# Expert MLP pieces of half the size placed by VectorE's time; the last MLP's bias moved to GpSimd

## Chip, cores and metric

The kernel runs on one core of a Trainium2 chip. The metric is the device time of one execution in microseconds, start to end; lower is better. The engines are called as the profile calls them: PE is TensorE's matmul (PEld its weight loads), DVE is VectorE, ACT is ScalarE, POOL is GpSimd, SP is the engine that issues most transfers.

## The reference, cut to what matters

The program is a chain of blocks over 4096 rows of 256 numbers: a Mamba block, causal attention, a SwiGLU MLP, a routed mixture of 8 experts, banded attention and a last MLP with GELU, with layer norms between. Two blocks are touched by the change in earnest:

```
def balanced_assignment(scores):           # T = 4096 rows, E = 8 experts, C = 512 rows each
    taken = zeros(T, bool)
    for e in range(E):
        s = where(taken, -inf, scores[:, e])
        _, idx = top_k(s, C)               # expert e takes its best C rows of those left
        parts.append(idx); taken = taken.at[idx].set(True)
routed = feat[sort_by_expert].reshape(E, C, D)
h = gelu(layer_norm(routed) @ w1[e] + b1[e]) @ w2[e] + b2[e]      # 256 -> 1024 -> 256, per expert
out = (routed + h) put back in row order
...
h = gelu(x @ w1 + b1, approximate=False)   # the last MLP, 256 -> 1024 -> 256, all rows
x = layernorm(x + (h @ w2 + b2))
```

## The kernel before

Rows lie in 32 tiles of 128 (X), worked through in 8 chunks of 512 rows (NC = 8, TPC = 4 tiles each). Matmuls are in float32. The stages run one after the other with a barrier of all engines between them: Mamba, causal attention, SwiGLU MLP (stage_mlp, kind "swiglu"), routing with the experts (stage_route), banded attention, last MLP (stage_mlp, kind "gelu").

**Routing.** Expert e's 512 rows are found by a search on DVE, expert after expert, since each leaves out the rows taken before it. A search goes in 12 steps (ASKS); in each, DVE makes a small count per partition and *asks* PE to sum it over the partitions with a small matmul (tell, line 2417; ask, line 2257), then waits for the answer (the wait on told). The 12 are: four counting questions and a pick (take_above), again four and a pick, one for ties, one for ranks (rank_taken). Behind the rank DVE builds one-hot arrays (lines 2310 and 2316), POOL multiplies two of them (one_hots), PE turns them into the list of rows with 64 small matmuls ("ids", line 2448), DVE copies the list out (copy_ids), SP writes it to memory and reads it back as indices, POOL gathers the rows with four indirect transfers (gather), and PE may start the expert's MLP: 8 transposes ("turn"), 8 pieces "up" (each two matmuls of 512 columns, behind each a GELU on ACT), and for each of the four tiles of rows two pieces "down" (each four matmuls of 256 columns), whose sum DVE takes with the bias ("out", add_bias). SP loads an expert's weights when the MLP two experts before it is done, and only then passes to that expert's list.

So PE has two jobs at once: it answers the questions of one search and computes the MLPs of earlier experts. It takes its instructions strictly in the order of the program, and that order is made by hand in ExpertPlan (line 1963). Time there is counted in questions: expert e's MLP begins 7.5 questions into the search after its own and its 17 pieces are spread evenly over 12 questions. DVE runs the acts "copy" and "out" that the plan puts between two questions right behind asking and before it waits for the answer (meanwhile).

**The last MLP.** Per chunk, PE transposes (transpose, line 1905), does 8 "up" groups into two PSUM banks with a GELU on ACT behind each, transposes the next chunk, and does for each tile 8 matmuls of 256 columns and a ninth of one row, ones_row times b2, that adds the bias (line 1941). DVE copies the rows of X into hn ahead of each chunk (rows, line 1810), adds the MLP's result to X (line 1842) and does the layer norm's sums; ACT and DVE finish the norm one chunk later. Chunks are two written out, a loop over pairs (Fori), two written out (chunks, line 1653), in the SwiGLU MLP too. At the start PE waits for the biases, transposes them (line 1899), waits for both weights and only then transposes the first chunk.

Of the kernel before, what the change touches and what calls it, by code (L numbers as in the profile page):

```python
# [46 lines left out]
E = 8  # L47
# [1556 lines left out]
def stage_mlp(k, kind):  # L1604
# [11 lines left out]
    with ExitStack() as ctx:  # L1616
# [13 lines left out]
        if not swiglu:  # L1630
            nb = E if expert else 1
            b1r = sb(tag + "_b1r", [nb * NF, P], F32)
            b1 = sb(tag + "_b1", [P, nb * NF], F32)
            b2 = sb(tag + "_b2", [1, nb, D], F32)
            ones_row = sb(tag + "_ones", [1, P], F32)
        if not gelu:
            gb = sb(tag + "_gb", [P, 2, KD], F32)
        hn = sb(tag + "_hn", [P, 2, TPC, D], F32)
# [4 lines left out]
        (w_in, b_in, b_T, ones_set, hn_ready, hnT, hT_ready, up, silu, G_ready, down, x_sum, x_out,  # L1643
         var_ready, std_ready, renorm, freed, combined, stat) = k.sems(
            tag, "w_in b_in b_T ones hn_ready hnT hT_ready up silu G_ready down x_sum x_out "
# [19 lines left out]
        with nc.Block() as block:  # L1665
            @block.sync
            def _(sp):
# [26 lines left out]
                if gelu:  # L1694
                    sp.dma_start(b1r[:, :], a["L1_ffn_b1"].rearrange("(f p) -> f p", p=P))\  # L1695
                        .then_inc(b_in, 16)
                    sp.dma_start(b2[:, 0, :], a["L1_ffn_b2"].rearrange("(one d) -> one d", one=1))\
                        .then_inc(b_in, 16)
# [53 lines left out]
            def _(act):  # L1752
# [7 lines left out]
                if not swiglu:  # L1760
# [30 lines left out]
                transposed(0, 0)  # L1791
                chunks(act, body)
# [6 lines left out]
            def _(dve):  # L1799
# [10 lines left out]
                def rows(c, u):  # L1810

                    for j in range(TPC):
                        tile = TPC * c + j
                        if swiglu:
                            ins = normalised(dve, k, hn[:, u, j, :], tile)
                        else:
                            ins = dve.tensor_scalar(hn[:, u, j, :], X[:, tile, :], 1.0, None,  # L1817
                                                    ALU.mult)
                        ins.then_inc(hn_ready, 1)

                def body(c, it, u, first, last):
                    for f in range(NF):
# [4 lines left out]
                        if f == 3 and not last and not expert:  # L1827
# [3 lines left out]
                    for j in range(TPC):  # L1831
# [9 lines left out]
                        else:  # L1841
                            ins = dve.tensor_tensor(X[:, tile, :], src, X[:, tile, :], ALU.add)  # L1842
# [23 lines left out]
                if not expert:  # L1866
# [27 lines left out]
            def _(pe):  # L1894
                pe.sem_inc(down, 8)
                if not swiglu:
                    pe.wait_ge(b_in, 16 * (4 if expert else 2))
                    pe.wait_ge(ones_set, 1)
# [3 lines left out]
                if not expert:  # L1902
                    pe.wait_ge(w_in, 16 * (3 if swiglu else 2))

                def transpose(c, it, u):
                    if expert:
                        pe.wait_ge(rows_in[u], 16 * it + 16)
                    else:
                        pe.wait_ge(hn_ready, TPC * c + TPC)
                    for kd in range(KD):  # L1910
                        for j in range(TPC):
                            mm = pe.transpose(PS[:, 4 + kd, P * j:P * j + P],  # L1912
                                              hn[:, u, j, P * kd:P * kd + P], k.ident[:, :])
                        mm.then_inc(hnT, 1)

                def body(c, it, u, first, last):
# [17 lines left out]
                    for j in range(TPC):  # L1934
                        pe.wait_ge(x_out, TPC * c + j + 7)
                        dst = PS[:, 6 + j % 2, 0:D]
                        for f in range(NF):
                            mm = pe.matmul(dst, G[:, f, P * j:P * j + P], w2[u][:, f, :],  # L1938
                                           start=(f == 0), stop=(f == NF - 1 and swiglu))
                        if not swiglu:  # L1940
# [4 lines left out]
                transpose(0, 0, 0)  # L1945
                chunks(pe, body)
# [16 lines left out]
class ExpertPlan:  # L1963


    def __init__(self):
        acts = []
        for e in range(E):
            told = ASKS * (e + 1) if e < E - 1 else ASKS * (E - 1) + 1
            begin, unit = ASKS * (e + 1) + 7.5, ASKS / 17  # L1970
            acts += [(told + 2.5, "ids", e), (told + 2.6, "copy", e), (begin, "turn", e)]
            acts += [(begin + unit * (1 + f), "up", e, f) for f in range(NF)]
            for j in range(TPC):
# [574 lines left out]
```

## Time and profile before

| what | us |
|---|---|
| median of three executions (4169.05 to 4177.55) | 4175.17 |
| the profiled execution | 4178.09 |
| its span, first to last instruction | 4176.3 |
| of it the SwiGLU MLP, 2354 to 2717 | 363 |
| routing and experts, 2717 to 3169.6 | 452.6 |
| last MLP, 3896.9 to 4176.3 | 279.4 |

| busy in | PE | DVE | ACT | POOL | granted clock |
|---|---|---|---|---|---|
| whole span | 3479.3 (83%) | 2425.5 (58%) | 1680.8 (40%) | 1143.2 (27%) | 0.927 |
| SwiGLU MLP | 342.8 | 106.4 | 69.9 | 22.1 | 0.97 |
| routing and experts | 308.7 | 234.8 | 83.2 | 87.4 | 0.84 |
| last MLP | 259.8 | 50.9 | 71.6 | 0.2 | 0.96 |

The times are busy times of an engine within the stretch; a granted clock of 1.00 is 2.4 GHz at PE, 0.50 is 1.2 GHz. In the two MLP stages one engine, PE, is busy almost throughout. In the routing stage none is.

### The profile page before, as it was taken

The numbers are of one execution on the slowest core, as the hardware profiler recorded it, in microseconds if no ns is written. First come the engines' busy times: TensorE is split into PE (matmuls) and PEld (weight loads), VectorE is DVE, ScalarE is ACT, GpSimd is POOL, SyncE is SP. The second block draws the span as 40 slices with busy tenths as digits, with TensorE's granted clock in tenths as the row PEclk, the third lists the DMA queues.
The fourth block names the chain that finished last, engine by engine and source line by source line (L and its number), as shares of the span: only waits on it lengthen the run. The fifth ranks groups of instructions, "written<-read, shape, count | busy, mean of one in ns | idle before, by whom it ended". The sixth has DMA issues, their size and how long they took to land. (4 is left out here: it accounts for less than half of the span.)

```text
span 4176.3 us, 47591 instructions
## 1 busy us (share of the span) xinstructions
PE 3479.3 (83%) x17329; PEld 1741.4 (42%) x17329; DVE 2425.5 (58%) x4104; ACT 1680.8 (40%) x2670; POOL 1143.2 (27%) x975
## 2 busy tenths in 40 slices
PE   6889999986579989999899799938883778778799
PEld 2334433332233333333333265614551455456465
DVE  2999999999457767677677133265613233344212
ACT  4655555554214545555555412111122334334222
POOL 2667677667321001220000000001222223211000
PEclk9999999999879999999999899969996889889799
DMA  2222222222231111211120100021222854653100
GB/s 78 71 67 70 68 69 68 67 69 72 51 59 35 22 30 32 41 36 29 28 37 7 46 16 10 5 97 56 70 71 86 150 95 91 120 82 51 32 15 20
DMA packets 210060, 232.04 MB, mean 56 GB/s; under 512 B 58695, under 2 KB 160408, under 8 KB 208524
## 3 DMA queue, kind: packets, MB, share of 16 engines
q1 hardware_dynamic: 206764, 220.72, 23.0%
q0 software_dynamic: 3072, 8.39, 0.6%
q8 instruction: 134, 2.20, 0.2%
q14 instruction: 90, 0.74, 0.1%
HBM read 183.13 MB, written 45.89 MB: 55 GB/s over the span
## 5 line engine op out<-in xcount | busy, mean ns | idle before, releaser
L1365 DVE TENSOR_REDUCE g_mxp<-PS 128x1 f32<-128x512 f32 (+3 forms) x1280 | 722.6, 606 | 222.2 <-PE PS L1511 122.0
L1237 ACT ACTIVATE g_pT<-PS 128x1024 f32<-128x1024 f32 (+3 forms) x640 | 552.4, 894 | 474.6 <-PE PS L1526 279.1
L379 POOL TENSOR_TENSOR WB<-m_dtx,WB 128x1024 f32<-128x1024 f32 x256 | 601.0, 2351 | 294.3 <-DVE WB L523 260.1
L411 ACT ACTIVATE PS<-m_dt,m_A 128x512 f32<-128x512 f32 x512 | 353.1, 691 | 431.0 <-DVE WB L514 430.4
L1503 PE MATMUL PS<-g_KT,WB 96*128 96x512 bf16 (+3 forms) x1280 | 429.3, 363 | 105.9 <-DVE g_mxp L1365 92.9
L608 PE MATMUL PS<-WB,ident 128*128 128x512 f32 x1024 | 503.0, 615 | 0.0
L514 DVE TENSOR_TENSOR_SCAN WB<-PS,m_state,WB 128x512 f32<-128x512 f32 x384 | 469.9, 1263 | 14.9 <-ACT PS L411 14.8
L1526 PE MATMUL PS<-WB,g_KT 99*128 99x512 bf16 (+3 forms) x1280 | 358.1, 352 | 1.2 <-ACT g_pT L1237 0.6
L1503 PEld LDWEIGHTS PS<-g_KT,WB 96*128 96x128 bf16 x1280 | 116.9, 98 | 480.6 <-DVE g_mxp L1365 400.9
L523 DVE TENSOR_TENSOR WB<-WB,PS 128x1024 f32<-128x1024 f32 x256 | 306.2, 1196 | 7.2 <-DVE WB L514 2.6
L1545 PE MATMUL PS<-g_pT,WA 128*32 128x512 f32 (+3 forms) x2560 | 300.9, 542 | 0.6 <-ACT g_pT L1237 0.6
L1365 DVE TENSOR_REDUCE w_mxp<-PS 128x2 f32<-128x512 f32 (+1 forms) x256 | 170.8, 670 | 217.8 <-PE PS L1511 215.4
L1237 ACT ACTIVATE w_pT<-PS 128x512 f32<-128x512 f32 (+2 forms) x352 | 159.7, 470 | 307.9 <-PE PS L1532 307.4
L608 PEld LDWEIGHTS PS<-WB,ident 128*128 128x128 f32 x1024 | 201.2, 196 | 175.3 <-issue 164.3
L1927 PE MATMUL PS<-s_hT,WA 128*128 128x512 f32 x512 | 223.3, 597 | 1.0 <-ACT s_hT L1769 1.0
L594 PE MATMUL PS<-m_bc,m_sel 96*128 96x512 bf16 x256 | 100.3, 392 | 120.3 <-DVE WB L523 119.9
L1526 PE MATMUL PS<-WB,w_KT 99*128 99x256 bf16 (+2 forms) x704 | 143.4, 251 | 65.1 <-DMA WB<-w_dm 65.0
L1392 DVE TENSOR_TENSOR X<-X,PS 128x512 f32<-128x512 f32 x128 | 88.0, 687 | 173.7 <-PE PS L1565 173.6
L514 DVE TENSOR_TENSOR_SCAN WB<-PS,WB 128x512 f32<-128x512 f32 x128 | 149.0, 1204 | 23.5 <-POOL WB L379 16.8
L1526 PEld LDWEIGHTS PS<-WB,g_KT 99*128 99x128 bf16 x1280 | 119.0, 99 | 96.3 <-ACT g_pT L1237 26.1
L1207 POOL TENSOR_TENSOR g_On<-g_Ot,g_rden 128x512 f32<-128x512 f32 x32 | 40.6, 1269 | 409.8 <-DMA g_rden<-g_dn 409.8
L1503 PE MATMUL PS<-w_KT,WB 96*128 96x192 bf16 (+2 forms) x704 | 136.2, 257 | 19.2 <-DMA w_V<-w_dv 18.2
(309 smaller groups left out, 5360.2 us busy)
## 6 DMA issues: line engine op xcount, KB each, us to landing
WB<-b_rows SPq DMA_DIRECT2D x256, 256.0 KB, 3.2
WB<-in_L_ffn_w SPq DMA_DIRECT2D x18, 1024.0 KB, 7.6
WB<-g_dq SPq DMA_DIRECT2D x96, 128.0 KB, 3.9
WB<-w_dq SPq DMA_DIRECT2D x96, 128.0 KB, 7.7
w_KT<-w_dk SPq DMA_DIRECT2D x96, 128.0 KB, 8.4
g_rden<-g_dn SPq DMA_DIRECT2D x128, 64.0 KB, 2.0
w_dv<-WA SPq DMA_DIRECT2D x8, 1024.0 KB, 4.7
w_V<-w_dv SPq DMA_DIRECT2D x16, 512.0 KB, 12.1
```

The source lines that it names most:

```text
L379: pool.tensor_tensor(hh[:, g % RING, :, :], dtx[:, MB * h:MB * h + MB, :], Bs[:, g % BRING, :].unsqueeze(1) .broadcast_to([P, MB, CH]), AL ...
L411: act.activation(PS[:, 2 + b, :], dt[:, c % 2, m, :], ACT.Exp, scale=Aneg[:, n, m:m + 1]).then_inc(dA_ready, 1)
L514: dve.tensor_tensor_scan(hh[:, g % RING, b, :], PS[:, 2 + b, :], hh[:, g % RING, b, :], first, ALU.mult, ALU.add)\
L523: dve.tensor_tensor(hC[:, g % 2, :, :], hh[:, g % RING, :, :], PS[:, 4, :].unsqueeze(1).broadcast_to([P, MB, CH]), ALU.mult).then_inc(hc, 1)
L594: pe.matmul(PS[:, 4, :], sel[:, n, :], bc3[:, c % 2, :], start=True, stop=True)\
L608: mm = pe.matmul(PS[:, b, :], k.ident[:, :], hC[:, g % 2, b, :], start=False, stop=False, skip_group_check=True)
L1237: act.activation(pT[:, n % 2, 2 * pair:2 * pair + 2, 0:width], PS[:, 2 * pair:2 * pair + 2, at:at + width], ACT.Exp, scale=DH ** -0.5).the ...
L1365: dve.tensor_reduce(mxp[:, q % 6, i % QB, hh:hh + per, k0 // CH if causal else 0], PS[:, 4 + m % 2, :].rearrange("p (h n) -> p h n", h=per ...
L1503: mm = pe.matmul(bank[:, lo - k0:hi - k0], QT[0:KS, u % QRING, h, P * (i % QB):P * (i % QB) + P], KT[0:KS, region(s, lo // CH), kmap(h), l ...
L1526: mm = pe.matmul(bank[:, at:at + width], KT[:, region(s, j // QB), kmap(h), P * (j % QB):P * (j % QB) + P], QT[:, chunk(q) % QRING, h, at: ...
L1545: mm = pe.matmul(PS[32 * hh:32 * hh + 32, 6, at:at + width], V[:, region(s, j // QB), j % QB, kmap(4 * g + hh), :], pT[:, n % 2, hh, 0:wid ...
L1927: mm = pe.matmul(PS[:, bank, :], w[:, kd, P * f:P * f + P], hT[:, u, kd, :], start=(kd == 0), stop=(kd == KD - 1))
```

## The change

1. ExpertPlan counts in microseconds. The 12 questions of a search get distances of their own (2.6, 1.7, 2.9, ... 6.8; together 32.5); an MLP's pieces are spread over one such search by their length, starting 17.0 into the search after the expert's own; "ids" goes 8.2 behind the rank question. An "up" piece is one matmul of 512 columns (it was two), a "down" piece is two of 256 columns (it was four). The number of matmuls, questions and copies is the same.
2. In the last MLP the bias matmul and ones_row are gone. b2 is loaded broadcast to all partitions, and POOL adds it to X, tile by tile, once the chunk's transposes have read X; DVE's addition waits for that (x_sum).
3. In the last MLP PE transposes straight from X; DVE's copies into hn and the waits on them are gone.
4. In the last MLP and the SwiGLU MLP PE waits for the weights behind the first chunk's transposes instead of before them; in the last MLP the biases' transpose stands behind them too, and ACT waits for b1 only then.
5. In the same two stages the eight chunks are all written out, without a loop.

```
-            for u in range(2):
-                body(u, 0, u, u == 0, False)
-            with eng.Fori(1, NC // 2 - 1) as it:
-                for u in range(2):
-                    body(2 * it + u, it, u, False, False)
-            for u in range(2):
-                body(NC - 2 + u, NC // 2 - 1, u, False, u == 1)
+            for c in range(NC):
+                body(c, c // 2, c % 2, c == 0, c == NC - 1)
...
+                if gelu:
+                    pool.wait_ge(b2_in, 16)
+                    with pool.Fori(0, NC) as c:
+                        pool.wait_ge(hnT, KD * c + KD)
+                        for j in range(TPC):
+                            pool.tensor_tensor(X[:, TPC * c + j, :], X[:, TPC * c + j, :],
+                                               b2[:, 0, :], ALU.add).then_inc(x_sum, 1)
...
                         else:
+                            dve.wait_ge(x_sum, TPC * c + j + 1)
                             ins = dve.tensor_tensor(X[:, tile, :], src, X[:, tile, :], ALU.add)
...
-                        if not swiglu:
+                        if expert:
                             mm = pe.matmul(dst, ones_row[:, :], b2[:, c if expert else 0, :],
                                            start=False, stop=True)
...
                 transpose(0, 0, 0)
+                if gelu:
+                    small()
+                if not expert:
+                    pe.wait_ge(w_in, 16 * (3 if swiglu else 2))
                 chunks(pe, body)
...
+        step, pick = 2.6, 1.7
+        pace = [step] * (len(STEPS) - 1) + [pick, 2.9] + [step] * (len(STEPS) - 1) + \
+            [pick, 1.5, 2.3, 6.8]
+        slot = sum(pace)
+        begin = slot + 17.0
+        works = [("turn", 1.1)]
+        works += [("up", 0.86)] * (2 * NF)
+        works += [("down", 0.86)] * (4 * TPC)
+        whole = sum(w for _, w in works)
         for e in range(E):
...
+            told = slot * (e + 1) - pace[-1] if e < E - 1 else slot * (E - 1) + 1.0
+            acts += [(told + 8.2, "ids", e), (told + 8.3, "copy", e)]
+            p, count = begin + slot * e, {}
+            for what, w in works:
...
+                p += w * slot / whole
...
-                        e, f = x
-                        if f == 0:
+                        e, f, kd = x
+                        if f == 0 and kd == 0:
...
-                        for f in range(NF // 2 * h, NF // 2 * h + NF // 2):
+                        for f in range(NF // 4 * h, NF // 4 * h + NF // 4):
                             mm = pe.matmul(PS[:, 6 + j % 2, 0:D], G[:, f, P * j:P * j + P],
```

## Rows read from the trace of the kernel before

**Rows 1.** windows of the searches and two after (us, busy by engine, PEclk, DMA)
```profile
core 0: us, PE busy (x) PEld busy (x) DVE busy (x) ACT busy (x) POOL busy (x), PEclk, DMA share, GB/s
2767.87:2797.43 29.56, 3.21 (x15) 2.07 (x15) 23.03 (x77) 0.00 (x0) 1.15 (x1) 0.50 0.00 0
2797.43:2834.96 37.53, 19.59 (x111) 10.26 (x111) 24.44 (x78) 6.27 (x8) 7.15 (x7) 0.61 0.05 15
2834.96:2875.11 40.15, 33.28 (x184) 20.98 (x183) 25.60 (x81) 6.94 (x10) 6.88 (x7) 1.00 0.21 66
2875.11:2917.80 42.69, 36.16 (x184) 22.16 (x183) 25.60 (x81) 6.94 (x10) 10.80 (x11) 0.92 0.22 74
2917.80:2959.10 41.30, 34.78 (x184) 21.52 (x183) 25.59 (x81) 6.94 (x10) 11.26 (x11) 0.96 0.24 77
...
3000.50:3041.80 41.30, 34.75 (x184) 21.61 (x183) 25.61 (x82) 6.94 (x10) 10.79 (x11) 0.96 0.23 77
3041.80:3068.57 26.77, 23.54 (x203) 17.64 (x203) 6.71 (x17) 2.06 (x3) 11.96 (x12) 0.94 0.11 31
```
**Rows 2.** timeline of PE behind the last question (start us, length us, ..., [idle])
```profile
3068.57 1.04 PE L2378 MATMUL PS<-ident,r_hn 128*128 128x128 f32 x8
3070.71 14.00 PE L2465 MATMUL PS<-r_hT,WB 128*128 128x512 f32 x32 [1.10 <-ACT r_hT L2173]
3085.49 14.08 PE L2476 MATMUL PS<-WB,WA 128*128 128x256 f32 x64 [0.78 <-ACT WA L2178]
3099.41 1.04 PE L2378 MATMUL PS<-ident,r_hn 128*128 128x128 f32 x8
```
**Rows 3.** timeline of PE between questions of one search, not consecutive
```profile
2838.06 0.18 PE L2433 MATMUL PS<-r_count,r_onesb 128*128 128x15 bf16 x1 [2.96 <-DVE r_count L2275]
...
2843.19 2.00 PE L2476 MATMUL PS<-WB,WA 128*128 128x256 f32 x8 [0.78 <-ACT WA L2178]
...
2845.12 0.19 PE L2448 MATMUL PS<-r_hot_col,r_hot_own 128*17 128x32 bf16 x1
...
2846.82 1.99 PE L2476 MATMUL PS<-WB,WA 128*128 128x256 f32 x8
```
**Rows 4.** timeline of DVE: questions of the first search and the same ones
```profile
2769.95 0.23 DVE L2276 TENSOR_SCALAR r_hit<-PS,r_one 128x15 f32<-128x15 f32 x1 [0.29 <-PE PS L2433]
...
2772.31 0.23 DVE L2276 TENSOR_SCALAR r_hit<-PS,r_one 128x15 f32<-128x15 f32 x1 [0.29 <-PE PS L2433]
...
2835.96 1.35 DVE L2269 SCALAR_TENSOR_TENSOR r_reach<-r_key,r_one,r_grid 128x480 bf16<-128x480 f32 x1
...
2838.95 0.72 DVE L2269 SCALAR_TENSOR_TENSOR r_reach<-r_key,r_one,r_grid 128x480 bf16<-128x480 f32 x1
...
2845.24 0.23 DVE L2276 TENSOR_SCALAR r_hit<-PS,r_one 128x15 f32<-128x15 f32 x1 [2.53 <-PE PS L2433]
```
**Rows 5.** timeline of SP and PE: an expert's list and its first use
```profile
2807.67 0.25 SPq L2091 DMA_DIRECT2D r_listed<-r_ids  x1
...
2817.76 1.97 PE L2378 MATMUL PS<-ident,r_hn 128*128 128x128 f32 x8 [0.88 <-DMA r_hn<-sorted,r_idx]
```
**Rows 6.** timeline of PE in the final MLP, end of the first chunk
```profile
3935.51 3.72 PE L1938 MATMUL PS<-WB,f_G 128*128 128x256 f32 x16
3939.79 3.72 PE L1938 MATMUL PS<-WB,f_G 128*128 128x256 f32 x16
3944.06 14.00 PE L1927 MATMUL PS<-f_hT,WB 128*128 128x512 f32 x32
```
**Rows 7.** timeline at the start of the final MLP
```profile
3896.88 0.91 SPq L187 DMA_DIRECT2D WB<-in_L_ffn_w  x2
...
3905.12 0.27 PE L1899 MATMUL PS<-ident,f_b1r 8*128 8x8 f32 x1 [21.42 <-DMA f_b<-in_L_ffn_b]
...
3909.17 17.02 PE L1927 MATMUL PS<-f_hT,WB 128*128 128x512 f32 x32 [0.69 <-ACT f_hT L1767]
```
**Rows 8.** line 1726 of the SwiGLU MLP (min/median/max ns)
```profile
L1726 POOL TENSOR_TENSOR s_io<-s_io,X x32: 722/725/730, 2367.1 to 2635.3; 128x256 f32<-128x256 f32 x32
```

More of the change, by code:

```diff
@@ L1759, in _ @@
                     act.wait_ge(b_in, 16 * (4 if expert else 2))
-                if not swiglu:
+                if expert:
                     act.wait_ge(b_T, 2)
@@ L1826, in body @@
                                               ALU.mult).then_inc(G_ready, 1)
-                        if f == 3 and not last and not expert:
+                        if f == 3 and not last and swiglu:
                             rows(c + 1, 1 - u)
@@ L1864, in renormalise @@
                         dve.wait_ge(renorm, TPC * c + TPC)
-                if not expert:
+                if swiglu:
                     rows(0, 0)
@@ L1895, in _, with small @@
                 pe.sem_inc(down, 8)
-                if not swiglu:
-                    pe.wait_ge(b_in, 16 * (4 if expert else 2))
-                    pe.wait_ge(ones_set, 1)
+                def small():
+                    pe.wait_ge(b_in, 16 * (4 if expert else 1))
+                    if expert:
+                        pe.wait_ge(ones_set, 1)
                     pe.transpose(PS[:, 7, 0:nb * NF], b1r[:, :], k.ident[0:nb * NF, 0:nb * NF])\
@@ L1901, in _ @@
                     pe.wait_ge(b_T, 2)
-                if not expert:
-                    pe.wait_ge(w_in, 16 * (3 if swiglu else 2))
+                if expert:
+                    small()
                 def transpose(c, it, u):
@@ L1938, in body @@
                             mm = pe.matmul(dst, G[:, f, P * j:P * j + P], w2[u][:, f, :],
-                                           start=(f == 0), stop=(f == NF - 1 and swiglu))
-                        if not swiglu:
+                                           start=(f == 0), stop=(f == NF - 1 and not expert))
+                        if expert:
                             mm = pe.matmul(dst, ones_row[:, :], b2[:, c if expert else 0, :],
@@ L1966, in __init__ @@
     def __init__(self):
-        acts = []
-        for e in range(E):
[L1969 to L1973, printed above, removed]
-                acts += [(begin + unit * (9 + 2 * j + h), "down", e, j, h) for h in range(2)]
-                acts.append((begin + unit * (10 + 2 * j) + 0.05, "out", e, j))
-        acts += [(g, "ask", g) for g in range(ASKS * (E - 1) + 1)]
+        step, pick = 2.6, 1.7
+        pace = [step] * (len(STEPS) - 1) + [pick, 2.9] + [step] * (len(STEPS) - 1) + \
+            [pick, 1.5, 2.3, 6.8]
+        assert len(pace) == ASKS
+        slot = sum(pace)
+        acts, at = [], 0.0
+        for g in range(ASKS * (E - 1) + 1):
+            acts.append((at, "ask", g))
+            at += pace[g % ASKS]
+        begin = slot + 17.0
[3 more added lines that the diff above has]
+        whole = sum(w for _, w in works)
+        for e in range(E):
+            told = slot * (e + 1) - pace[-1] if e < E - 1 else slot * (E - 1) + 1.0
+            acts += [(told + 8.2, "ids", e), (told + 8.3, "copy", e)]
+            p, count = begin + slot * e, {}
+            for what, w in works:
+                i = count[what] = count.get(what, -1) + 1
+                if what == "turn":
+                    acts.append((p, "turn", e))
+                elif what == "up":
+                    acts.append((p, "up", e, i // 2, i % 2))
+                else:
+                    acts.append((p, "down", e, i // 4, i % 4))
+                    if i % 4 == 3:
+                        acts.append((p + 1.0, "out", e, i // 4))
+                p += w * slot / whole
         self.order = [a[1:] for a in sorted(acts, key=lambda a: a[0])]
```

45 lines of the change are left out of this document (23 added, 22 removed).

## The prediction

> **What bounds the kernel now.** I read three views in this order: busy time and granted clock by stretch, to see which engine is full in which stage; the timelines of PE and DVE within one search, to see who waits for whom; and the last MLP's timeline. The profiled execution took 4178.09 us (span 4176.3), 2.9 above the median of 4175.17; the sum below is made against the former and then moved to the latter.
>
> In the last MLP PE is the bound: its matmuls follow each other without a gap [rows 6], so every matmul taken away there shortens the end by its own length. In the routing stage nobody is full. The first search, with no MLP beside it, takes 29.56 us; the one with the first MLP's beginning 37.53; then they take 40.15, 42.69 and three times 41.3 to 41.4 (the first and the last stand there), with DVE busy only 25.6 and PE 33 to 36 of it [rows 1]. The reader is to see the pattern in the rows: undisturbed, a question is answered 0.29 after DVE asked and the questions are 2.36 apart; with an MLP beside it DVE stands 2.53 for the same answer [rows 4], since PE works off "down", "ids" and the rest in program order first [rows 3]. A little before, PE stood 2.96 waiting for a question [rows 3]. Each waits for the other in turn. Behind the last question an MLP takes PE 30.84 us [rows 2], so neither engine needs 41.
>
> **The plan, part by part.** *Prices.* An "up" group of two matmuls is 14.00/8 = 1.75 us, and the piece of one half of it; I take 0.86. The 32 "down" matmuls of an MLP take 13.92, a quarter-tile piece 0.87; a turn is 1.04, behind it PE waits 1.10 for ACT, and 0.78 before the first "down" for the last GELU [rows 2] (counted from the matmul's issue 1.3 and 1.0). "ids" is 1.70 (from 2845.12 to 2846.82) [rows 3]. The work is unchanged; halving the pieces adds no instruction, and the semaphore counts stay.
>
> *Walk of a steady search.* I sorted the new plan's times and set PE's pieces in each gap beside what DVE needs in it. DVE's gaps, from question to question, are those of the first search's twelve, all within the 29.56 of its row: 2.36 between counting questions, 1.5 to a pick, 2.8 behind it, 1.2 to the ties, 2.6 to the ranks, about 7 to the next search. The new pieces: in the 7 us gap seven "up" (6.0, fits). Between the first and the second question one "up", the 1.0 for the GELU, a "down", "ids" and a "down": 0.86 + 1.0 + 0.87 + 1.70 + 0.87 = 5.3 against 2.36, an excess of 2.9. Then two "down" (none); three against 2.36 (0.3); two against 1.5 (0.3); three against 2.8 (none); two (0.1); two and the turn, 2.8 against 2.36 (0.4); two "up" behind the turn's wait of 1.3, 3.0 against 1.5 less what PE was early (0.7); two against 1.2 (0.3, and 0.7 for the ties' answer, which also waits); two against 2.6 (0.1). These are 5.1 to 5.8, I take 5.1 beyond the free answers, as the early question carries over. To this comes what POOL costs DVE: beside POOL's one-hot work the first step of a search takes 1.35 where the same step later takes 0.72 [rows 4], and the one before it is stretched alike: 1.25. So the new search is 29.56 + 1.25 + 5.1 = 35.9. DVE's four additions and the copy lie behind asking, under the answer, as now.
>
> The same walk with the old plan gives excesses of 9.0 and 39.8, where the one search at full clock took 40.15 [rows 1]; I add the missing 0.4 and get 36.3. Bounds: nothing below 29.56 + 1.25 = 30.8, which would need every question free; above, the 40.15 of today, if the waits only change places.
>
> *Clock.* Of the searches only the one of 40.15 had a granted clock of 1.00; in the others it was 0.92 to 0.96 [rows 1], which is PE at 1.2 GHz for a part, and each is 1.1 to 2.5 longer. The idle of 2.96 before the first question [rows 3] comes with it, though it stood ahead of the search at 1.00 too. In the new order PE has no gap over about 1.3 in a search, so I take these losses as gone. TensorE: Matmul & The Clock Gate (the Trainium skill), section "HAM oscillation", says that a matmul engine left waiting between bursts falls back to half rate and pays the rise anew each time. By that rule the loss goes with the gaps, as in the sum; if instead it stayed as in these rows, the five searches would be some 7 longer.
>
> *Sum of the routing stage.* Five searches: 40.15 + 42.69 + 41.30 + 41.40 + 41.30 = 206.8 against 5 x 36.3 = 181.5: -25.3. The one before them carries the first MLP's beginning with a clock of 0.61 [rows 1]; it keeps that and gains what the walk gives, -3. Behind the last search, the time to the next turn was 26.77, with PE at 0.94 [rows 1]; now it is the last "up" pieces and question (3.4), 0.86 + 1.0, sixteen "down" (13.9) and two "ids" (3.4): 22.6, -4. Two whole MLPs of 30.84 follow unchanged, and the stage's end. Together -32.5.
>
> *What must come in time.* From SP's write of a list to the gathered rows at PE it takes 2817.76 - 2807.67 = 10.1 us [rows 5]. In the new plan the copy is about 14 before the turn; 4 are left. For the seventh expert I get 2.7. SP passes to a list behind the load of weights issued some 16 earlier, POOL's scatters are two experts old: both hidden. If a list were later, PE would stand at the turn with the questions behind it, 1 us for 1 us.
>
> **The last MLP.** Four matmul groups of a chunk start 4.28 apart with the bias (3935.51 to 3939.79) [rows 6]; without one, 13.92/4 = 3.48 [rows 2]. So 0.80 x 32 tiles = -25.6. What is late next: nothing, as the groups' sums have two banks and DVE takes one in less than half a us; the GELUs run as now. POOL's four additions a chunk, at 0.725 each [rows 8], start when the chunk is transposed and are done in 2.9, where the first "down" sum comes 3.5 behind its own "down" start and a whole "up" phase of 14 [rows 6] lies between for all but the wait's first chunk; there b2 lands with the biases around 3905 and the sum is due some 17 later. DVE is busy 51 of 279 in this stage, so what POOL's port use costs it is covered.
>
> *Starts.* PE begins now at 3905.12 when the biases are in, and the "up" matmuls at 3909.17 [rows 7]. With copies, transposes and ACT ahead of the loads, 3905.7 is possible: -3.5. But the rise to full clock, which cost the first chunk 17.02 - 14.00 = 3.0 [rows 6, 7], may then start as late as the matmuls: between 0 and -3.5 is kept, more by +1.5; I take -2.3. The SwiGLU MLP's first transposes (2 us at that clock) likewise move ahead of its weights, though ACT still waits for the norm's columns behind them: 0 to -3, taken -1. Loops written out save under 0.1 a chunk: -0.6. The removed DVE copies were hidden by PE: 0.
>
> **Sum.** -32.5 - 25.6 - 2.3 - 1 - 0.6 = -62. On the profiled execution 4178.1 - 62 = 4116; on the median, 4175.2 - 62 = 4113.
>
> **Rivals.** (a) *The searches run at DVE's pace.* If the excess at "ids" is smaller than walked, a search comes to 32.5, near the sum of the plan's own distances: 5 x 3.8 more, 4094. For it: PE's need per search is 28.9 + 1.7 and the answers, about 32.5. Against it: "ids" and the GELU's wait fall into one short gap. (b) *The waits change places.* Pieces twice as fine still stand ahead of questions; if the clock still falls and each search stays at 39 to 40, the routing stage gives about 10 and the whole 4136. For it: PE is needed nearly 90% of the new search, so any lateness stays. (c) *Slower: the list comes late.* If a list needed more than the 14 us that the plan leaves, PE stands at each of seven turns. The price is its lateness times seven; it decides from 62/7 = 9 us beyond the margin, a list of 23 us where the row shows 10.1. At 12 us beyond, 4175 + 22 = 4197. (d) *The change doesn't do what it says in the last MLP*: the sum on DVE waits for POOL each time, as POOL waits for the transposes of the same chunk. Only if POOL took over 14 a chunk; rows say 2.9. It would give 4139.
>
> **How the numbers follow.** My forecast (4100 to 4127) 0.66; (a) 0.10; (b) 0.18; (c) 0.03; (d) 0.03. The likeliest is 4113. The range takes in (a) and (b) with the bounds of the starts and the clock: 4092 to 4138. A measurement of this kernel tells about 0.2% (8 us) from no change; faster by more holds in all but (c) and a bad (b): 0.95, within 0.02, slower 0.03.
>
> **What the changed profile would show.** Searches of about 36 with a granted clock of 1.00 and PE busy near 90%; DVE's longest wait, about 3, at the second question; no wait of PE for gathered rows except at the first MLP. In the last MLP, no row of line 1941, chunks of 28.7 instead of 31.9, and DVE waiting for PE, not POOL, at its sums. The prediction is wrong if PE stands at turns, if the clock in the searches stays at 0.96, or if a chunk of the last MLP is over 29.

## The result, and the profile after

The changed kernel takes 4116.92 us (median of four executions, 4114.76 to 4124.66); the kernel before took 4176.36 beside it on the same chip (4169.05 to 4188.65). The ratio is 0.9859, with a 95% interval of 0.9838 to 0.9879. The profiled execution took 4114.76, its span is 4112.9 and its mean granted clock 0.931 (0.927 before). Forecast were 4113.

Where the time went is best read by stage. Each stage is measured from its own first transfer issue to that of the next, in the profiled executions (so the routing stage before is 2722.39 to 3169.66, less than the rounder stretch of the section on the time before):

| stage | before | after | change | the prediction's step |
|---|---|---|---|---|
| all up to the SwiGLU MLP's first load | 2353.9 | 2353.1 | -0.8 | none |
| SwiGLU MLP | 368.5 | 368.2 | -0.3 | -1 |
| routing and experts | 447.3 | 422.5 | -24.8 | -32.5 |
| banded attention (not touched) | 727.2 | 720.1 | -7.1 | none |
| last MLP | 279.4 | 249.1 | -30.3 | -28.5 |

First the windows over the seven searches, as in [rows 1]; the last two rows are the stretch from the last search to the next turn, and one whole MLP.

```profile
core 0: us, PE busy (x) PEld busy (x) DVE busy (x) ACT busy (x) POOL busy (x), PEclk, DMA share, GB/s
2765.60:2795.15 29.55, 3.22 (x15) 2.06 (x15) 23.02 (x77) 0.00 (x0) 1.18 (x1) 0.50 0.00 0
2795.15:2828.82 33.67, 18.97 (x112) 10.04 (x113) 24.45 (x78) 6.28 (x8) 7.08 (x7) 0.64 0.06 16
2828.82:2865.12 36.30, 33.24 (x185) 20.88 (x184) 25.77 (x82) 6.95 (x10) 7.00 (x7) 1.00 0.23 73
2865.12:2902.78 37.66, 33.42 (x185) 20.91 (x184) 25.75 (x82) 6.95 (x10) 10.84 (x11) 1.00 0.25 84
2902.78:2940.27 37.49, 33.42 (x185) 20.90 (x184) 25.83 (x82) 6.94 (x10) 10.91 (x11) 1.00 0.25 85
...
2977.78:3015.21 37.43, 33.37 (x184) 20.86 (x183) 25.83 (x81) 6.95 (x10) 10.85 (x11) 1.00 0.25 85
3015.21:3042.66 27.45, 23.78 (x204) 18.02 (x203) 6.76 (x17) 2.06 (x3) 12.75 (x12) 0.94 0.13 40
3042.66:3073.49 30.83, 28.95 (x106) 19.01 (x104) 1.70 (x4) 6.95 (x10) 10.70 (x11) 1.00 0.34 116
```

The searches that took 40.15 to 42.7 now take 36.3 and four times about 37.5, PE is busy 33.2 to 33.4 of them and its clock is 1.00 in each. The first of the five is the 36.3 of the prediction; the other four are 1.2 longer, and the stretch behind the last search is not shorter than before (27.45 for 26.77). Both are followed up below.

Next VectorE's timeline at the second question of that first search (start us, us, engine line op, tiles; in brackets the idle time ahead and what ended it), the place where the walk put its largest excess:

```profile
2832.11 0.23 DVE L2304 TENSOR_SCALAR r_hit<-PS,r_one 128x15 f32<-128x15 f32 x1 [0.28 <-PE PS L2461]
...
2833.54 0.66 DVE L2303 TENSOR_REDUCE r_count<-r_reach 128x15 bf16<-128x480 bf16 x1
2836.67 0.18 DVE L2266 CAST r_ids<-PS 17x32 uint32<-17x32 f32 x1 [2.48 <-PE PS L2476]
2837.74 0.23 DVE L2304 TENSOR_SCALAR r_hit<-PS,r_one 128x15 f32<-128x15 f32 x1 [0.89 <-PE PS L2461]
...
2840.09 0.23 DVE L2304 TENSOR_SCALAR r_hit<-PS,r_one 128x15 f32<-128x15 f32 x1 [0.28 <-PE PS L2461]
```

The question is asked at 2834.20 and answered at 2837.74: 3.5 us, against 0.28 for the first and the third question. DVE's copy of the ids between them shows the reason: PE was at "down", "ids" (L2476) and "down" first.

The last MLP, its start (PE's timeline) and its sums (groups of DVE and POOL):

```profile
3872.12 0.27 PE L1902 MATMUL PS<-ident,f_b1r 8*128 8x8 f32 x1 [6.16 <-DMA f_b1r<-in_L_ffn_b]
3872.66 16.48 PE L1932 MATMUL PS<-f_hT,WB 128*128 128x512 f32 x32 [0.26 <-DVE f_b L1814]
```

```profile
L1844 DVE TENSOR_TENSOR X<-PS,X 128x256 f32<-128x256 f32 x32 | 13.5, 422 | 92.4 <-PE PS L1943 92.4
L1720 POOL TENSOR_TENSOR X<-X,f_b 128x256 f32 x32 | 22.2, 732 | 196.7 <-PE PS L1917 169.7 <-DMA f_b<-in_L_ffn_b 27.1
```

The first "up" starts 8.8 us behind the stage's first load where it started 12.3 behind it [rows 7]; DVE's sums wait for PE alone. From the second on, the chunks start 28.6 apart where they were 31.9 apart.

### The profile page after: what moved, and what is told of

The parts are those of the page before. It is cut to its first block and busy times, and to the rows that moved or that the text cites. A ratio compares the mean times of both kernels' runs of the same rounds, so it can differ in the third digit from the quotient of the medians.

```text
span 4112.9 us, 47062 instructions
## 1 busy us (share of the span) xinstructions
PE 3444.2 (84%) x17265; PEld 1730.6 (42%) x17265; DVE 2419.5 (59%) x4072; ACT 1681.5 (41%) x2670; POOL 1166.4 (28%) x1006
## 5 line engine op out<-in xcount | busy, mean ns | idle before, releaser
L1932 PEld LDWEIGHTS PS<-s_hT,WA 128*128 128x128 f32 x512 | 98.3, 192 | 129.1 <-issue 128.8
```

What stands on the lines that cost most here:

```text
L1932: mm = pe.matmul(PS[:, bank, :], w[:, kd, P * f:P * f + P], hT[:, u, kd, :], start=(kd == 0), stop=(kd == KD - 1))
```

## The experiments

All edits are to the changed kernel unless said otherwise. "Routing stage" is from its first load to that of the banded attention, in the run's profile; the median of all the run's executions stands beside it, with that of the kernel before in the same comparison.

**1. One part at a time.** The plan with the MLP stages as before:

> The routing stage as in the changed kernel, all MLP stages as before. Theory (the two parts add up, and the plan is worth what the traces of the stage show): the stage takes 422 to 424 us where the kernel before had 447.3, searches of 37.5 at a granted clock of 1.00, the last MLP stays at 279 and the time is 4176.4 - 25 = 4151. The banded attention behind it, which the change doesn't touch, was 727.2 in the kernel before and 720.1 in the changed one. If those 7.1 belong to the plan (the stage finds PE in another state), they come here too and the time is 4144. If they are chance from one execution to the next, they can be here or not in the profile, and the time stays near 4151. Rival (the parts help each other through the clock or the loads): the gain is under 20.

Measured: 4144.31 (before 4177.66; ratio 0.9912, 0.9891 to 0.9933), routing stage 422.4, last MLP 279.2. The MLP stages with the plan as before:

> The MLP stages as in the changed kernel, the plan of the experts as before. Theory: the last MLP takes 249 instead of 279.4, the SwiGLU stage 368.2, searches stay at 40 to 43 with a clock of 0.92 to 0.96; the time is 4176.4 - 30.3 - 1 = 4145. If the 7.1 of the banded attention belong to the MLP stages, 4138. Rival: part of the 30.3 came from what PE had done before, then under 25 here, 4151 or more.

Measured: 4139.38 (ratio 0.9904, 0.9881 to 0.9927), routing stage 451.5, last MLP 249.1, SwiGLU stage 368.3.

By the stages the parts add up: 24.9 and 30.3, and the changed kernel has 24.8 and 30.3. By the medians they are 33.4 and 38.3, together 71.7 where the changed kernel gains 59.4; each of the three has an interval of 8 to 10 us to either side, so the medians neither confirm nor refute the sum. The routing stage of the old plan, the same instructions, took 447.3 in one execution and 451.5 in this one, so this stage is not known better than to some 4 us either. The banded attention, the same instructions in all of them, took 727.2, 720.1, 715.6 and 718.1 in these four profiled executions, and 716.9 to 730.2 in the ten below, with no order by kernel. So its -7.1 is nobody's gain, and from here on the stages decide and the medians only back them.

**2. The time axis or the half size?** Two kernels with the MLP stages as before; each has one part of the new plan. The first keeps the time axis and puts both halves of a piece at one place:

```diff
-        works += [("up", 0.86)] * (2 * NF)
-        works += [("down", 0.86)] * (4 * TPC)
+        works += [("up", 1.72)] * NF
+        works += [("down", 1.72)] * (2 * TPC)
...
-                    acts.append((p, "up", e, i // 2, i % 2))
+                    acts += [(p, "up", e, i, kd) for kd in range(2)]
...
-                    acts.append((p, "down", e, i // 4, i % 4))
-                    if i % 4 == 3:
-                        acts.append((p + 1.0, "out", e, i // 4))
+                    acts += [(p, "down", e, i // 2, 2 * (i % 2) + h) for h in range(2)]
+                    if i % 2:
+                        acts.append((p + 1.86, "out", e, i // 2))
```

> The plan's time axis with pieces of the old size (two matmuls of an up, four of a down at one place); MLP stages as before. Theory A (the axis does it): what stands ahead of a question is settled by the sum of the work in a gap; a walk of PE and DVE with the prediction's prices gives 36.0 per search where the half pieces give 35.9, so searches of 37.5 and the same time as with half pieces, within 3 us. Theory B (the size does it): a whole piece stands 0.86 us longer ahead of a question, at about half of the twelve questions of a search: 4 to 5 us a search more, 41 to 42, no gain over the kernel before and 20 to 25 slower than the half pieces.

The second lays half pieces evenly over the questions' numbers, as the old plan did with whole ones; "ids", turn and questions stand as in the old plan:

```diff
+            begin, unit = ASKS * (e + 1) + 7.5, ASKS / 17
+            for f in range(NF):
+                acts += [(begin + unit * (1 + f + kd / 2), "up", e, f, kd) for kd in range(2)]
+            for j in range(TPC):
+                acts += [(begin + unit * (9 + 2 * j + h / 2), "down", e, j, h) for h in range(4)]
+                acts.append((begin + unit * (10.5 + 2 * j) + 0.05, "out", e, j))
...
```

> Half pieces laid out evenly by the number of the question, as before, not by time; MLP stages as before. Theory A (the axis does it): about as many pieces stand in the gap of 1.5 us as in that of 7, the walk gives 39.1 per search plus 0.4, so 39.5 at full clock and up to 41.5 where the clock falls in the long gap; the time is 4168 to 4176. Theory B (the size does it): searches of 37.5 and the time of the half pieces on the time axis, about 4151.

Measured: whole pieces on the time axis 4149.1 (ratio 0.9925, 0.9898 to 0.9951) with a routing stage of 420.3; half pieces on the question axis 4176.14 (ratio 0.9999, 0.9983 to 1.0015) with one of 451.8. One steady search of each, in windows with the columns above:

```profile
2909.62:2946.04 36.42, 33.02 (x184) 21.04 (x183) 25.61 (x81) 6.95 (x10) 11.73 (x11) 1.00 0.27 87
```

```profile
2958.60:3000.00 41.40, 34.90 (x183) 21.61 (x183) 25.78 (x84) 6.97 (x10) 11.61 (x11) 0.96 0.23 77
```

The axis (with the ids' place on it) is the whole gain of the plan; halving the pieces alone gives nothing. Whole pieces on the time axis took 420.3 for 422.4, but no answer was late in their profile (experiment 5), and late answers cost the halves 4.8: without late answers a search with half pieces takes 36.3, one with whole pieces 36.4. The change's title names the half size first; the prediction gave it no price of its own, and the walk had not needed it. What counts is how much work stands in a gap beside the gap's length. The clock goes with it: in the second kernel, with more idle time of PE, it is 0.96 as in [rows 1].

**3. The bias back on TensorE**, with the rest of the last MLP as changed:

```diff
-                        if expert:
+                        if not swiglu:
                             mm = pe.matmul(dst, ones_row[:, :], b2[:, c if expert else 0, :],
                                            start=False, stop=True)
...
```

POOL's additions and DVE's wait for them are out, and ones_row is back.

> The changed kernel with the last MLP's bias added by TensorE's matmul again, in everything else as changed (order of the last MLP's start, transposes read from X, loops written out). Theory: each of the 32 tiles costs 0.80 us of TensorE again, chunks of 31.8 instead of 28.6, the last MLP takes 249.1 + 25.6 = 274.7, and of the difference to the kernel before (279.4) the rest of 4 to 5 is the start and the loops; the time is about 4117 + 25.6 = 4142. Rival (the bias matmul was cheaper than the 0.80 read off the starts, and the start and the loops gave more): under 20 more than the changed kernel, below 4137.

Measured: 4145.01 (before 4180.26; ratio 0.9910, 0.9896 to 0.9923), last MLP 275.1. PE's timeline in it:

```profile
3900.18 3.72 PE L1938 MATMUL PS<-WB,f_G 128*128 128x256 f32 x16
3903.83 0.69 PE L1941 MATMUL PS<-f_b,f_ones 1*128 1x256 f32 x2
3904.45 3.72 PE L1938 MATMUL PS<-WB,f_G 128*128 128x256 f32 x16
```

So the bias is 275.1 - 249.1 = 26.0 (0.81 a tile), and the start with the loops 279.2 - 275.1 = 4.1.

**4. The lists' margin.** The turns 8 us of the plan's time earlier (`begin = slot + 9.0` for 17.0):

> The changed kernel with each MLP's turn laid 8 us (of the plan's time) earlier against the searches: begin = slot + 9 for slot + 17. The prediction's margin for the list was 4 us. Theory (the list's way of about 10 us is the limit, and the questions stand in the queue behind TensorE's wait): TensorE waits 3.7 us for the gathered rows at each turn, the walk gives 39.1 instead of 35.9 per search, the routing stage 18 longer; with 1.2 a search of late answers gone or not, 4130 to 4140. Rival (the wait is covered by the slack of the answers): searches of 37.5 stay and the time within 4 us of 4117. If the list takes longer than 10.1, more by its lateness times seven.

Measured: 4166.27 (ratio 0.9962, 0.9945 to 0.9979), routing stage 472.0, 49.5 longer, searches of 45.7 to 47.2. One search in windows, and PE's timeline in it:

```profile
2922.04:2968.60 46.56, 37.15 (x185) 22.82 (x184) 25.95 (x82) 7.07 (x10) 11.19 (x10) 0.85 0.21 69
```

```profile
2936.21 1.11 PE L2504 MATMUL PS<-WB,WA 128*128 128x256 f32 x4
2944.64 1.97 PE L2406 MATMUL PS<-ident,r_hn 128*128 128x128 f32 x8 [7.32 <-DMA r_hn<-sorted,r_idx]
2946.40 0.23 PE L2453 MATMUL PS<-r_pick,r_onesb 128*128 128x32 bf16 x1
```

PE stands 7.3 at the turn, not 3.7, with the question of L2453 behind it. SP's queue tells why:

```profile
2930.48 0.25 SPq L2119 DMA_DIRECT2D r_listed<-r_ids  x1
2931.74 0.35 SPq L2122 DMA_DIRECT2D r_idx<-r_listed  x1
2937.35 0.38 SPq L2106 DMA_DIRECT2D WB<-in_L_ffn_w  x1
2937.77 0.47 SPq L2107 DMA_DIRECT2D WB<-in_L_ffn_w  x1
```

From the list's write to the rows at PE it is 2944.64 - 2930.48 = 14.2, not the 10.1 of [rows 5]: the load of 2 MB of weights, which now goes out before the gathered rows are in, runs beside the gathers. The same run tells it apart from the scatters: its first list, with no load beside it, took 9.9 (2796.91 to 2806.82), its second, with a load but before the first scatter, 13.8. And behind the idle time the clock is 0.85, so the pieces in front of the next questions take longer. Both costs were missing in the theory; the direction and the mechanism (the questions behind the waiting turn) were right. The cliff that the prediction's rival (c) spoke of is real, and 8 us of the plan's time away it costs 49.5, not 18. Rival (c)'s price, the lateness once for each of seven turns, fits: PE's seven waits there are 5.0 to 9.3 long and add up to 51.7.

**5. The late answers.** In each of the four searches of 37.5 two answers come late, the sixth and the seventh. DVE's timeline at the sixth question of one of them, then POOL's and PE's:

```profile
2957.94 0.66 DVE L2303 TENSOR_REDUCE r_count<-r_reach 128x15 bf16<-128x480 bf16 x1
2960.03 0.23 DVE L2304 TENSOR_SCALAR r_hit<-PS,r_one 128x15 f32<-128x15 f32 x1 [1.43 <-PE PS L2461]
```

```profile
2956.59 1.01 POOL L2158 DMA_INDIRECT hidden<-r_io,r_idx  x1 [0.30 <-issue]
2957.90 0.99 POOL L2158 DMA_INDIRECT hidden<-r_io,r_idx  x1 [0.30 <-issue]
2959.19 0.97 POOL L2158 DMA_INDIRECT hidden<-r_io,r_idx  x1 [0.30 <-issue]
```

```profile
2958.66 0.18 PE L2461 MATMUL PS<-r_count,r_onesb 128*128 128x15 bf16 x1
2958.69 1.97 PE L2504 MATMUL PS<-WB,WA 128*128 128x256 f32 x8
```

PE's matmul for that question starts at 2958.66, 0.06 behind the question's end, and takes 0.18; the answer is used 1.37 after its start where 0.22 is usual. PE was not late, and it went straight on with the next "down"; the signal was late. The trace's semaphore record says so itself: the update that DVE waits for is stamped 2960.00, and that of the "down" matmul ahead of the question, which started at 2958.37, came with it (2959.97). It happens while POOL issues an expert's scatters, the indirect transfers that put its results back, which exist from the fourth search on. The scatters moved behind the one-hot work:

```diff
-                    if e >= 3:
-                        scatter(e - 3)
                     if e < E - 1:
                         one_hots(e)
+                    if e >= 2:
+                        scatter(e - 2)
...
```

> The changed kernel, with GpSimd's four scatter transfers of an expert issued behind the one-hot work of the search before, about 10 us before they stand now, and so no longer straight behind the four gathers. In the changed kernel, from the fourth search on, TensorE's answer reaches VectorE 1.4 to 1.6 us after its matmul's start where it takes 0.22 elsewhere, while those scatters are issued; that is 1.2 us a search, and the last list's matmuls are slowed in the same way. Theory A (the row of eight indirect transfers on GpSimd delays TensorE's semaphore updates): the late answers are gone, searches of 36.3, the stage behind the last search 5 us shorter, in all 8 to 10 us less in the routing stage, 412 to 414 instead of 422.5. Theory B (each scatter delays what is signalled just then, wherever it stands): the late answer moves to another question, searches of 37.5 stay. Theory C (it has nothing to do with GpSimd): questions 6 and 7 stay late as they are.

Measured: 4116.49 (ratio 0.9841, 0.9826 to 0.9856), routing stage 419.1, the four searches 36.6 to 36.7 with no late answer. The second question waits 0.4 longer, since the ids beside a scatter take 2.1 for 1.76. So moving them took the lateness away, as theory A said, in this one profile. The stretch behind the last search is as long as it was, against theory A, so that of its 8 to 10 us 3.4 came.

There the last ids are slow. PE's groups between 3029.6 and 3034.1 of the changed kernel:

```profile
L2476 PE MATMUL PS<-r_hot_col,r_hot_own 128*17 128x32 bf16 x32 | 2.2, 176 | 0.9 <-issue 0.9
L2476 PE MATMUL PS<-r_hot_col,r_hot_tile 128*17 128x32 bf16 x32 | 2.1, 176 | 1.2 <-issue 1.2
```

They were laid later:

```diff
-            acts += [(told + 8.2, "ids", e), (told + 8.3, "copy", e)]
+            late = 0.0 if e < E - 1 else 12.0
+            acts += [(told + late + 8.2, "ids", e), (told + late + 8.3, "copy", e)]
```

> The changed kernel with only the last expert's ids (64 short matmuls) and their copy laid 12 us later, behind the turn of the seventh expert. In the changed kernel they took 4.37 us where the other seven took 1.76, with four indirect transfers issued by GpSimd in the same time; in other runs 2.1 with one beside them and 5.5 with five. That is what kept the stretch from the last search to the next turn at 27.45 where the prediction had 22.6. Theory A (GpSimd's indirect transfers slow TensorE's short instructions): the ids take 1.76 again, and the stretch loses their 1.7 (moved) and the stalls: 3015 to 3042.7 becomes 23 to 24; the routing stage is 2.5 to 3.5 shorter, since the ids' own 1.8 come back behind the turn. Theory B (two blocks of ids stand too near each other for the supply of instructions): here they are 18 us apart, the same result, but with the first downs of that stretch slow as well. Theory C (the place in the stage, whatever stands there): still 4 us or more. The whole time changes by less than its runs differ, so the trace decides.

Measured: 4106.6 (before 4172.99; ratio 0.9833, 0.9811 to 0.9855), routing stage 412.5, 10.0 less. The same group, and a window from the last search on, which runs 3.4 past the next turn:

```profile
L2477 PE MATMUL PS<-r_hot_col,r_hot_own 128*17 128x32 bf16 x32 | 1.7, 176 | 0.0
```

```profile
3010.23:3034.00 23.77, 21.89 (x150) 16.81 (x149) 7.06 (x17) 3.51 (x5) 12.74 (x12) 1.00 0.20 52
```

The ids take 1.76 again and the next turn (3030.65) comes 20.4 behind the last search for 27.45; 1.76 of the 7 come back behind it. That was more than expected, since the clock there is 1.00 for 0.94, too. Theory B of this run, two blocks of ids too near each other, is ruled out by the kernel before: its last two blocks start 5.9 apart (8.8 in the changed kernel) and took 1.76 and 1.75. Unexpected: all four searches took 36.35 with no late answer, with the scatters in their old place. Whether the ids' place did it was asked by a second execution of that routing stage, with the MLP stages as before:

> The run with the last ids laid 12 us later had searches of 36.35 without one late answer, although the scatters stand where they stood in the changed kernel (37.5). This is the same routing stage once more, with the MLP stages as before, so a second execution of the same stage. Theory A (the place of the last ids decides, by what lies in TensorE's and GpSimd's programs): 36.35 again in every search, a routing stage of 412 to 413. Theory B (the late answers come and go with the execution, as they were 0.7 to 1.6 in three executions of the changed plan): at least one search of 36.8 to 37.5, the stage 413 to 417. In both the last ids take 1.76, for no transfer of GpSimd stands beside them; the time 4176 - 35 = 4141 to 4137 by the medians.

Measured: 4146.73 (before 4177.12; ratio 0.9932, 0.9906 to 0.9957), routing stage 417.8, the four searches 37.49 to 37.65, and the last ids 1.76. Its median gives nothing away, as the runs spread by 21 us. So theory A is out: the same routing stage, instruction for instruction, had no late answer in one profile and late answers in all four searches in the other. Whether they come and go with the execution, as theory B has it, or with what else the program holds, is not shown, for each kernel was profiled once. The last ids, in their new place, took 1.76 in both.

**6. The walk as a planner.** Other distances in the time axis, found by trying many axes in the prediction's walk:

```diff
-        pace = [step] * (len(STEPS) - 1) + [pick, 2.9] + [step] * (len(STEPS) - 1) + \
-            [pick, 1.5, 2.3, 6.8]
+        pace = [1.6, 2.75, 2.75, 1.35, 3.45, 2.7, 1.5, 2.4, 1.55, 1.8, 2.5, 7.0]
-        begin = slot + 17.0
+        begin = slot + 15.9
-            acts += [(told + 8.2, "ids", e), (told + 8.3, "copy", e)]
+            acts += [(told + 7.5, "ids", e), (told + 7.60, "copy", e)]
```

> The changed kernel with other numbers in its time axis only: the distances between the questions of a search are 1.6, 2.75, 2.75, 1.35, 3.45, 2.7, 1.5, 2.4, 1.55, 1.8, 2.5, 7.0, the ids come 7.5 behind the last question instead of 8.2, and the turn 15.9 into the slot. They were found by running the prediction's walk of TensorE and VectorE over many such axes and keeping the one that ends first. Theory (the walk is right, the excess of 3.3 us at the second question is only the placing of ids): searches of 33.1 + 0.4, with no answer over 1.1 us late, the routing stage 15 us shorter, 4100 to 4103. Rival A (late answers of 1.2 us a search stay and grow with the stage's density): 4105 to 4108. Rival B (the walk fitted the shown order only, and what it can't see takes the place of the removed waits): searches stay at 36 to 37.5, 4112 or more.

Measured: 4099.87 (before 4180.26; ratio 0.9806, 0.9792 to 0.9819), routing stage 410.0, the first steady search 33.58, the four others 34.6 to 34.75 with the late answer. The median is next to the theory's 4100, but the stage is 12.5 shorter where the theory had 15: the walk's search came true (33.5 forecast), and so did the late answers of rival A. Then all three edits, and all but the moved scatters:

> The changed kernel with three edits together: the tuned distances of the run before, the scatters moved off the gathers, and the last ids late. Theory (they add up): searches of 33.5 with no late answer, where the tuned distances alone had 34.6; four searches by 1.1, and 3 behind the last one: the routing stage 402 to 403 where the tuned distances alone had 410.0, and 7 less in time, 4093. Rival (the scatters, now beside the ids of each expert, cost there what they cost at the answers: in the run with the scatters moved each block of ids took 2.1 for 1.76 and the second question waited 0.4 longer): searches of 33.9 to 34.2, the stage 405 to 407, 4096.

> The tuned distances with the last ids late, but the scatters where the changed kernel has them: the version with all three edits (routing stage 397.2, searches of 33.58) less the moved scatters. If the scatters' place is what makes TensorE's answers late, searches of 34.6 come back in at least some of the four from the third on and the stage takes 399 to 402. If it was the last ids, or nothing is left of the lateness in this order, 33.6 throughout and 397 to 398. The time is within 4 us of the version with all three, 4087.

Measured: all three 4086.93 (before 4172.99; ratio 0.9804, 0.9790 to 0.9817), routing stage 397.2, 5 to 6 less than expected, since the stretch from the last search to the next turn fell by 8.5 (27.8 to 19.3), of which 3 were counted on. The rival did not come: with scatters beside them the ids took 1.76 here, not 2.1. Without the moved scatters 4098.01 (before 4177.12; ratio 0.9810, 0.9782 to 0.9837), routing stage 405.1, longer than the 399 to 402 expected; its four searches are 34.7 to 34.9. A steady search of the version with all three:

```profile
2925.08:2958.65 33.57, 32.52 (x184) 21.31 (x183) 25.69 (x82) 6.94 (x11) 11.12 (x10) 1.00 0.29 95
```

PE is busy 32.5 of 33.6; this order is at PE's pace. It is the fastest of all, 86 us below the kernel before and 23 to 30 below the changed one (23 by the two ratios, 30 by the medians; the routing stage is 25.3 shorter).

## Why the prediction was right, point by point

The time was right (4113 for 4116.92, 3.9 off; 62 less forecast, 59.4 less measured), and so was the mechanism in both parts. A part of the closeness is luck. In the profiled executions the stages that the change touches gave 55.4 of the 62, as two terms of the routing stage were wrong, and 7.9 that no step had came from stages that the change doesn't touch (7.1 of it the banded attention), so that the whole came to 63.3. None of the prediction's signs of being wrong showed: no turn waited, the clock in the searches was 1.00, a chunk of the last MLP took 28.6.

- **What bounds each stage**: right. By the stages the two parts are independent (experiment 1).
- **The steady search, 36.3**: right for the order as walked. 36.30 where no scatter runs, 36.35 in an execution without late answers, 3.3 of excess at the second question (3.54 less the free 0.28) where 2.9 was walked, and PE busy 33.2 of 36.3, the "near 90%". The same walk, with its 0.4 added, forecast other orders: 36.4 (36.4 to 36.5 measured; the expectation on record said 37.5, as it took the late answers in) and 33.5 (33.58) at full clock. Where the clock fell it was short: 39.5 (41.3 to 43.8) with half pieces on the question axis, and 39.5 (45.7 to 47.2) with the turns earlier, where the list's way was too short in it as well. The four searches with scatters beside them were 1.2 longer, because their answers' signals came late. That term was missing: 4.8 in sum.
- **Clock, losses taken as gone**: right, 1.00 in all five. In experiments 2 and 4, where PE was left waiting, it was 0.96 and 0.85. That a matmul engine left waiting between bursts goes back to half rate is what TensorE: Matmul & The Clock Gate (the Trainium skill), section "HAM oscillation", states, and the traces agree in both directions.
- **The search before them, -3**: 37.53 to 33.67, -3.9.
- **Behind the last search, 26.77 to 22.6**: wrong, 27.45. The step priced the second ids at 1.7, from a row without POOL's transfers beside it. They took 4.4, and the clock fell to 1.2 GHz for a while behind their stalls (at 3034.6), which makes the stretch's mean 0.94. With them out of the way the same pieces took 20.4 (22.6 less the ids' 1.7 is 20.9). These 4.9 and the 4.8 above are more than the 7.7 that the stage's sum was too large; the search before the five and the stage's ends gave the difference back.
- **The list's margin of 4**: held in the changed order, where PE never waits for gathered rows. But 10.1 was read from a list with no load of weights beside it; where the two meet it is 13 to 15 (experiment 4). The chance of 0.03 for rival (c) rested on a number that the change itself could have moved.
- **The bias, -25.6**: -26.0. Rival (d), DVE waiting for POOL, is ruled out by the row of L1844: all its 92.4 of waiting is for PE.
- **The last MLP's start, -2.3, and the loops, -0.6**: together -4.1 for -2.9. The first "up" comes 3.5 earlier against the stage's first load, as held possible, and the first chunk's 16.48 is no longer than the 17.02 of [rows 7]: the clock's rise was not paid a second time, so all of the 3.5 was kept.
- **SwiGLU, -1**: -0.3 in this pair of profiles, which one pair can't tell: the stage took 366.7 to 369.1 in the fourteen, 368.0 on average in the nine with this change and 368.8 in the five without. The transposes go first, but ACT's wait for the norm's columns sets the start, as the prediction named for the lower end.
- **Rival (a), DVE's pace**, did not come: the best order run here took 33.6 with PE busy 32.5 of it, so the rival's 32.5 would leave PE no wait at all. **Rival (b)** did not come as told, for the clock held and no search took 39. But lateness did take back 9.7 of the 32.5 that the prediction expected from the stage, by signals and stalls and not by pieces ahead of questions.

## What to carry to other kernels

Where two engines answer each other in program order, write down each one's work per gap beside the gap's length and walk it through; such a walk, set once against a search known at full clock, gave three new orders within 0.1 us a search where the clock stayed up and no signal came late, and found the best of them; where the clock fell it was 2 to 8 us a search too short. A finer cut of the work without its placing gave nothing. A price taken from a row holds only with the same neighbours: ask of each step which transfers will lie beside it in the new order. And a stage that was not touched tells how much of a difference is chance; compare the stages before crediting the whole.

## What the runs showed of the hardware

- POOL issues indirect transfers in rows of about 1 us each, 0.3 apart. Where the 64 short matmuls of an expert's ids ran on PE with four or five of them beside, they took 4.1 to 5.6 us (six blocks of six traces), with stalls for which the profile names only "issue"; moved away, the same block took 1.76 (four traces). With the last transfer of a row beside them they took 2.1 to 2.5 (five blocks of one trace). The other 101 blocks of the fourteen traces took 1.75 to 1.88. But eight of these had a transfer beside them as well: in three it began in the block's last half us, and in the version with all three edits the second of a row lay wholly inside in four of the five blocks, and nothing was lost. So what a transfer costs is not fixed by its being there, and which one does it stays open.
- Signals from PE to DVE can come late around POOL's scatters though PE's matmul starts on time: DVE goes on 1.3 to 1.8 us after its start for the usual 0.22 (0.7 to 0.8 at a seventh question behind a late sixth). With half pieces on the time axis and the scatters straight behind the gathers, all four searches had it in six profiles and none in a seventh; in the six it cost 0.5 to 1.3 us a search. With the scatters moved, none in two. With the old plan it was in all four searches of one kernel, at the eighth question (1.4 to 1.6 for 0.54), and in three of the four that question came 0.4 us after the last scatter's issue had ended, so it is not the issuing alone; the kernel before had it in none, with the same routing stage (447.3 for 451.5). With half pieces on the question axis one search of four had it (0.97 for 0.21). The runs with the turns earlier and with whole pieces had none. So the transfers' place takes part, but why the same stage has it in one kernel's profile and not in another's stays open.
- The same stage of the same instructions (banded attention) took between 715.6 and 730.2 us in fourteen executions of fourteen kernels. That spread is about half of the gain of either part of this change.
